# Nineteen pair numbers, loaded to registers at once instead of one by one

## The reference, cut to what matters

```
g = silu(h @ W[e].T); u = h @ W[e].T; y = (g * u) @ W[e].T      # h = layernorm(x)
x = x + tanh(g_xattn) * y                                       # y of the row's own expert
h2 = layernorm(x); logits = h2 @ Wr + br
# the two best of 8 small experts, each 512 -> 16 -> 512, with relu, weighted by softmax
x = x + tanh(g_ffn) * sum_e w[e] * (relu(h2 @ Wd[e] + bd[e]) @ Wu[e] + bu[e])
```

## Time and profile before

| | |
|---|---|
| median of 3 runs | 201.59 us |
| profiled execution | 201.35 us |
| its span | 199.6 us |
| TensorE busy | 173.2 us (87%) |
| VectorE busy | 154.8 us (78%) |
| ScalarE busy | 112.5 us (56%) |
| GpSimd busy | 100.5 us (50%) |

### The profile page before, as it was taken

One profiled execution on the slowest core, in us unless ns is written; L12 is line 12 of the kernel. 1 busy time (PEld: TensorE's weight loads), 2 busy tenths in 40 slices (PEclk: granted clock), 3 DMA queues, 4 the chain that ended last, 5 costly groups with the idle time before them and its releaser, 6 DMA issues.

```text
span 199.6 us, 4088 instructions
## 1 busy us (share of the span) xinstructions
PE 173.2 (87%) x1074; PEld 104.2 (52%) x1074; DVE 154.8 (78%) x442; ACT 112.5 (56%) x223; POOL 100.5 (50%) x246
## 2 busy tenths in 40 slices
PE   1655897999996989999999999999999999977560
PEld 1644473655553546656566565665656656534210
DVE  4868597697768798898988989787877878668640
ACT  2595599984395274573755737557375572445200
POOL 4477856417344474475744736416245162445641
PEclk9995599999999999999999999999999999999955
DMA  4937672100310101203001010010010100101121
GB/s 134 395 123 225 231 221 73 53 3 11 95 48 9 53 0 53 57 0 107 21 35 53 3 53 25 34 53 23 34 53 2 56 28 25 53 3 53 54 105 53
DMA packets 6789, 13.51 MB, mean 68 GB/s; under 512 B 2392, under 2 KB 2520, under 8 KB 6768
## 3 DMA queue, kind: packets, MB, share of 16 engines
q0 software_dynamic: 2560, 8.39, 12.8%
q1 hardware_dynamic: 4208, 4.86, 7.3%
HBM read 9.06 MB, written 4.19 MB: 66 GB/s over the span
## 4 chain that ended last, share of the span: by engine, by line
PE 68%; POOL 7%; DMA 7%; DVE 6%; issue 6%; ACT 2%; SPq 2%; POOLq 1%; DVEq 0%
PE ps_y L582 8%; PE ps_y L584 8%; PE ps_y L583 8%; PE ps_a L582 7%; PE ps_a L584 6%; PE ps_a L583 6%; DMA xs<-in_x_dram,rows_of 4%; PE ps_pT L603 4%; PE ps_h2T L664 3%; PE ps_hT L656 3%; DMA bu_nat<-in_L_ffn_bu_dram 2%; POOL hot_slot L411 2%; PE ps_o L621 2%; POOL xs L418 2%; PE ps_o L624 2%
## 5 line engine op out<-in xcount | busy, mean ns | idle before, releaser
L435 POOL TENSOR_SCALAR ve<-mv 128x1 f32<-128x1 f32 x32 | 7.6, 238 | 59.6 <-DVE mv L1067 50.1
L775 ACT ACTIVATE h<-xs,mrs,rs 128x512 f32<-128x512 f32 x16 | 21.0, 1312 | 19.4 <-POOL mrs L437 19.4
L762 ACT ACTIVATE pT_hi<-ps_pT 128x512 f16<-128x512 f32 x19 | 11.3, 594 | 36.1 <-PE ps_pT L603 36.1
L582 PE MATMUL ps_y<-w_hi,pT_hi 128*128 x76 | 28.8, 379 | 2.0 <-DVE w_lo L931 1.2
L582 PE MATMUL ps_a<-w_hi,hT_hi 128*128 x76 | 29.3, 386 | 0.7 <-DVE hT_lo L1044 0.6
L583 PE MATMUL ps_a<-w_lo,hT_hi 128*128 x76 | 29.3, 386 | 0.0
L584 PE MATMUL ps_a<-w_hi,hT_lo 128*128 x76 | 29.2, 384 | 0.0
L583 PE MATMUL ps_y<-w_lo,pT_hi 128*128 x76 | 28.8, 379 | 0.0
L584 PE MATMUL ps_y<-w_hi,pT_lo 128*128 x76 | 28.8, 379 | 0.0
L1056 DVE SCALAR_TENSOR_TENSOR xs<-ps_y,y_t,xs 128x512 f32 x19 | 14.3, 750 | 12.1 <-PE ps_y L584 11.4
L436 POOL TENSOR_TENSOR rs<-ve,neg_half 128x1 f32<-128x1 f32 x32 | 19.7, 615 | 2.7
(11 more groups left out here) (205 smaller groups left out, 418.9 us busy)
## 6 DMA issues: line engine op xcount, KB each, us to landing
w_nat<-in_ctx_dram SPq DMA_DIRECT2D x4, 1024.0 KB, 8.0
xs<-in_x_dram,rows_of POOLq DMA_INDIRECT x16, 3.6
wd_nat<-in_L_ffn_Wd_dram SPq DMA_DIRECT2D x1, 256.0 KB
wu_nat<-in_L_ffn_Wu_dram SPq DMA_DIRECT2D x1, 256.0 KB
out_dram<-xs,rows_of POOLq DMA_INDIRECT x16, 2.9
b_in<-in_L_ffn_bd_dram SPq DMA_DIRECT2D x1, 64.0 KB
bu_nat<-in_L_ffn_bu_dram SPq DMA_DIRECT2D x3, 16.0 KB
tok_i<-in_itok_BxS_dram SPq DMA_DIRECT2D x1, 8.0 KB, 1.7
```

The lines of the kernel that those rows point to most:

```text
L582: mm(ps[:, :], lhs_hi[:, kc, :], hi, start=(kc == 0), stop=False)
L775: a(h2[:, :, :], x1[:, col(k), :].rearrange("p o (q c) -> p c (o q)", c=KC), ACT.Identity, bias=mrs[:, 1, col(k)], scale=rs[:, 1, col(k)]) ...
```

## The change

All numbers of a table are loaded to registers by one call per engine and table, once: TensorE loads `expert_i` where it loaded its first number, ScalarE loads `pair_tile_i` ahead of its `step(-1, -1)`, and VectorE loads `pair_tile_i` and `source_i` between `router_bias()` and `step(1, 1)`. The steps then index Python lists of register values. The call states why the value can't be out of range, and no check at run time is made. Arithmetic on the registers for addresses stays where it was.

```diff
+        def all_of(eng, row, top, why):
+            _, values = nc.values_load_multi_w_load_instructions(
+                row, engines=(eng.engine,), min_val=0, max_val=top, skip_runtime_bounds_check_because=why)
+            return values
...
-            def expert_of(k):
-                return pe.value_load(expert_i[0:1, col(k)], min_val=0, max_val=E - 1)
...
             def experts_of(i, i0):
-                return (expert_of(i - 1) if some(NP, -1, i0) else None,
-                        expert_of(i) if some(NP, 0, i0) else None)
+                return (experts[i - 1] if some(NP, -1, i0) else None,
+                        experts[i] if some(NP, 0, i0) else None)
...
             pe.wait_ge(s_expert, 1)
-            experts_0 = experts_of(0, 0)
+            experts.extend(all_of(pe, expert_i[0:1, 0:NP], E - 1,
+                                  "a sum of E - 1 comparisons, each 0 or 1"))
             top_norms_T(2)
-            step(0, 0, experts_0, meanwhile=lambda: top_norm(2))
+            step(0, 0, meanwhile=lambda: top_norm(2))
             w_blocks(2)
             step(1, 1)
-            experts_2 = experts_of(2, 2)
...
-                    tile = (0 if k == 0 else
-                            act.value_load(pair_tile_i[0:1, col(k)], min_val=0, max_val=T - 1))
+                    tile = tiles[k] if k else 0
...
             act.wait_ge(s_places, 1)
+            tiles.extend(all_of(act, pair_tile_i[0:1, 0:NP], T - 1,
+                                "a pair's number less the groups that ended, at most T - 1 by the min"))
             step(-1, -1)
...
             def place(k):
-                return (dve.value_load(pair_tile_i[0:1, col(k)], min_val=0, max_val=T - 1),
-                        dve.value_load(source_i[0:1, col(k)], min_val=0, max_val=2 * T - 1))
+                return tiles[k], sources[k]
...
             router_bias()
             dve.wait_ge(s_places, 1)
+            tiles = all_of(dve, pair_tile_i[0:1, 0:NP], T - 1,
+                           "a pair's number less the groups that ended, at most T - 1 by the min")
+            sources = all_of(dve, source_i[0:1, 0:NP], 2 * T - 1, "a tile's number, or that plus T")
             dve.wait_ge(s_y_t, 1)
             step(1, 1, meanwhile=lambda: low_parts(2))
```

More of the change, by code:

```diff
@@ L626, in experts_of, with step @@
             def experts_of(i, i0):
-                return (expert_of(i - 1) if some(NP, -1, i0) else None,
-                        expert_of(i) if some(NP, 0, i0) else None)
-            def step(i, i0, experts=None, meanwhile=None):
+                return (experts[i - 1] if some(NP, -1, i0) else None,
+                        experts[i] if some(NP, 0, i0) else None)
+            def step(i, i0, meanwhile=None):
                 has_y, has_a = some(NP, -1, i0), some(NP, 0, i0)
-                e_last, e_now = experts or experts_of(i, i0)
+                e_last, e_now = experts_of(i, i0)
                 if has_y and not has_a:
@@ L678, in step @@
                        ident[:, :]).then_inc(wtT_done, 1)
+            experts = []
             step(-1, -1)
@@ L695, in rest_of_w3 @@
                 w_blocks(3, range(KC - 1, KC))
-            step(2, 2, experts_2, meanwhile=rest_of_w3)
+            step(2, 2, meanwhile=rest_of_w3)
             step(3, 3)
@@ L804, in step @@
                       bias=mrs[:, 0, col(tile)], scale=rs[:, 0, col(tile)]).then_inc(normed1, 1)
+            tiles = []
             act.wait_ge(s_pool, 1)
```

## The result

The changed kernel took 205.75 us in the median of 4 runs (206.91, 206.72, 204.77, 204.70) against 201.48 (201.31 to 201.91) before: a ratio of 1.021, 95% interval 1.0135 to 1.0285. A second set of 4 runs gave 206.48 (206.19 to 206.84), 1.0251 (1.0203 to 1.0300). The profiled execution is the one of 206.91, span 205.2.

What follows compares the result with a forecast made beforehand. TensorE was taken to bound the full steps, and a chain through the bu_nat transfer and VectorE the filling. VectorE's loads +2.65 us, removals 0, other loads covered: 201.35 to 204.0 profiled, 204.2 against 201.59; range 201.8 to 209.5.

Steps and rivals of the forecast that it cites:

- the case that the forecast rests on: Filling of the pipeline: small price per further word, 204.2 us (203 to 205.2), chance 0.42.
- Nothing comes back from what was removed.: All three engines: the old single loads and checks were hidden, so removing them gains 0.
- TensorE's load is hidden.: TensorE from 19.8 us: its load, 1.15 us plus first-load extra, ends near 21.1, before ps_a(0) at 22.46.
- VectorE's two loads are paid in full, between `router_bias` and `pT_low(0)`.: VectorE in the filling: two loads of 1.15 us plus first-load extra and gaps, uncovered, +2.65 us.
- the price of a further word: In each table load: 0.047 us per word beyond the first, 0.85 us for 18, taken from VectorE's ALU_OP.
- one trip: Rival on the table loads: all words come at the price of one, 0.30 us a load; +0.95, 202.5 us, chance 0.15.
- word by word: Rival on the table loads: each word costs a good part of a whole load; 205.2 us and up, chance 0.28.
- ScalarE's load is covered by the wait for `bu_nat`.: ScalarE from 20.8 us: hT_hi(0) 1.2 us late, covered by VectorE's 1.47 us wait for bu_nat.
- From `ps_y(0)` on everything moves by the same amount.: TensorE from ps_y(0), dense to 58 us: all moves with VectorE's 2.65 us; the steady step stays 8.29 us.
- The 0.40 stop may move off the chain: Rival, VectorE in add_y(3) at 58.23: fewer instructions shift the stop, giving back 0.40 us; not slower, chance 0.15.
- the signs by which the prediction would be wrong: Steady step changes length; ps_y(0) not delayed by what the two loads take; 0.40 stop gone, its time seen in the end.

Runs made afterwards that it cites:

- TensorE's part: The kernel before with only TensorE's table loaded at once (19 numbers), other engines loading singly with checks: 201.60 us, ratio 1.0003.
- the sizes: The kernel before with fifteen loads of 1 to 19 numbers added at the end of VectorE's queue; 1 word 311 ns, 19 words 1803; own time not compared.
- ScalarE's part: The kernel before with only ScalarE's table loaded at once (19 numbers), other engines loading singly with checks: 203.45 us, ratio 1.0073.
- `router_bias` moved: The kernel before with router_bias placed behind low_parts(2) within step(1, 1): 200.32 us, ratio 0.9955.

## Why the prediction was right, and which terms were mis-sized

The forecast was 204.2 us, the result 205.75: slower, in the range, and VectorE's two loads are the main cause, as named. The time lies above the 203 to 205.2 of the case that the forecast rests on. The range reached up to it for the sake of a rival, and 2.6 of the 5.6 us by which the span grew are terms that the forecast had at nothing. That the number came so near is in part luck. By its steps:

- **Nothing comes back from what was removed.** Right. No change with the checks alone removed (0.9998), none with TensorE's part (1.0003).
- **TensorE's load is hidden.** Right, at 2.02 us in place of 1.15: `ps_a(0)` starts 1.91 late, as much as `hT_hi(0)` on ScalarE (1.89), and in TensorE's own part it starts at 22.30 (22.46 before).
- **VectorE's two loads are paid in full, between `router_bias` and `pT_low(0)`.** Right in place, mis-sized in price: `pT_low(0)` follows `router_bias` 3.91 us later, and 0.10 before. The difference is 3.81, forecast 2.65. The failed term is the price of a further word, taken from an ALU_OP as 0.047 us. Over 0.304 for one word, nineteen at 1.80 come to 0.083 a word; by my reading of the sizes it is seven trips of 0.22 to 0.26 instead of eighteen register writes. By that reading the two rivals on the price each held for a part of the table: one trip for each group of four, word by word for the three left over.
- **ScalarE's load is covered by the wait for `bu_nat`.** Failed in part. With 1.88 us for the load and 1.36 of slower clock in `ps_a(0)`, `router_bias` came 0.97 later with its wait gone; in the second profile, with 0.61 of slower clock, only 0.09 later. ScalarE's part alone (1.0073) shows a second way, `pT_hi(0)`, that I had not followed.
- **From `ps_y(0)` on everything moves by the same amount.** Failed by a term that was in no sum, TensorE's clock. The wait for the loads opened a gap of 2.94 us, and behind it seven of the twelve matmuls of `ps_y(0)` took 0.427 us in place of 0.215. `ps_y(0)` to `ps_pT(1)` grew from 4.87 to 6.53 us. The trace of before had the hint in `ps_a(0)`, whose first matmuls behind a wait are 0.43 us apart and the later ones 0.215.
- **The 0.40 stop may move off the chain** (rival, not slower). It did, but alone it couldn't decide the sign. `add_y(3)` after, against the earlier trace rows:

```profile
64.47 0.09 DVEq L1059
64.56 0.03 issue
64.60 0.04 DVEq L1059
```

From `ps_pT(4)` to `ps_h2T(0)` it is 5.40 us in the kernel before and 5.39 to 5.40 in the four experiments that leave the number of VectorE's instructions ahead of this place as it was (ScalarE's part, TensorE's part, the loads at the end, `router_bias` moved), and 5.02 or 5.03 in the two profiles of the changed kernel and the seven experiments in which it is another. So it goes with what VectorE's queue holds ahead of this place (24 of its instructions have gone there and two have come, where the prediction counted only the 24). All seven experiments also lack VectorE's checks, and none changes the number and keeps the checks; against the checks as the cause speaks that `add_y(4)` has the same ones and a stop of 0.03. What happens there no run shows.

The sum as measured, against the profile of before: +0.97 `router_bias`, +3.81 the loads, -0.10 between `pT_low(0)` and `ps_y(0)`, +1.66 clock, -0.38 the stop, -0.02 up to `ps_pT(18)`, -0.34 in the end: +5.60, the growth of the span. The last term needs no cause in the change: from `ps_pT(18)` to the end it is 24.3 to 26.7 us in the thirteen profiles without additional loads there.

The rival that a word costs a good part of a load came nearer in time (206.8 for 2.1 us a table) than my own case, and its mark "loads of 2 us, L981 later than 31.7" is what the trace shows. Its band, 205.2 and up, holds the result, and it had chance 0.28. Of the signs by which the prediction would be wrong two came in part: `ps_y(0)` was delayed by 4.68 us where the two loads take 3.84, and the stop of 0.40 has gone and 0.38 of it is seen. The first is ScalarE's term above, the second the rival of the stop; neither shows another link than VectorE's queue.

**Open.** Why the first four executions of the changed kernel fall in two pairs, 204.7 and 206.8: no profile is of the faster pair, so that the clock's 1.66 us is the difference was only argued. The time of `ps_a(0)` and the end of the run vary by as much between profiles. Why `bu_nat` landed anywhere from 31.3 (TensorE's part) to 32.51 us (no checks) in the six profiles that show it waited for. Why `ps_a(0)` takes 2.70 to 4.49 us with the same work ahead of it: its clock was read from the matmul distances and not tested by itself.

## What to carry to other kernels

Replacing many short loads hidden in full steps by one long one in the filling moves sequencer time from where it is free to where it is paid (here nothing gained on TensorE, 1.0003, and 3.81 us paid on VectorE); ask which queue the long one blocks and who waits, before counting instructions saved. Load register tables early, on a queue that waits anyway, from the table's first word and padded to a multiple of four words (twenty words would be five trips, some 1.35 us as an estimate from the sizes, against 1.80 for nineteen; no run has tried it). Where the change opens a gap at TensorE, the matmuls behind it may cost more as well: 0.427 us each in place of 0.215 here, 1.66 us in all behind the gap of 2.94.

## What the hardware showed that was not expected

A load of registers is cheaper for four words than for three (357 and 998 ns), and for sixteen from number 0 than for sixteen from number 1 (1095 and 3603). Gaps of 2.09 to 5.71 us at TensorE were followed by some 3 to 6 us of matmuls at half speed (those of 512 columns 0.427 us apart), 1.66 to 2.9 us lost; the wait of 1.89 us ahead of `ps_y(0)` in the kernel without checks was not (4.87 us to `ps_pT(1)`). And the granted clock of a stretch can miss it: in this profile of the changed kernel 24 to 29 us has

```profile
24.00:26.00 2.00, 1.63 (x4) 0.64 (x5) 1.86 (x11) 2.00 (x4) 0.72 (x1) 1.00 0.38 77
```

with its matmuls 0.427 us apart, while the second profile of the same kernel shows 0.50 there with the same distances:

```profile
24.00:26.00 2.00, 1.75 (x5) 0.70 (x6) 1.86 (x11) 2.00 (x5) 0.60 (x1) 0.50 0.31 111
```
